# A decoder layer's down router: the hidden activations stored token by token and streamed, the router's table loaded as weights

## The reference

```
def kmoe(x_flat, W_router, A, B, scale, bias, d_in1, d_in2, d_out1, d_out2, top_k):
    logits = x_flat @ W_router.T                 # 64 experts
    vals, idx = jax.lax.top_k(logits, top_k)     # top_k = 2
    probs = jax.nn.softmax(vals, axis=-1)
    xs = x_flat.reshape(-1, d_in1, d_in2)
    Y = jnp.einsum('nkoi,nij,nkpj->nkop', A[idx], xs, B[idx])
    out = jnp.einsum('nkop,nk->nop', Y, probs).reshape(-1, d_out1 * d_out2)
    return out * scale + bias
...
h = kmoe(x_flat, W_up, A_up, B_up, scale_up, bias_up, 32, 32, 64, 64, 2)
h = jax.nn.gelu(h, approximate=False)
y = kmoe(h, W_down, A_down, B_down, scale_down, bias_down, 64, 64, 32, 32, 2)
```

## Time and profile before

| | |
|---|---|
| median of 3 runs | 1330.0 us (1328.71 to 1331.12) |
| the profiled execution | 1328.52 us |
| its span | 1326.8 us |
| mean granted TensorE clock | 0.972 |
| TensorE matmul busy | 1207.4 us, 91% |
| TensorE weight load busy | 968.3 us, 73% |
| ScalarE busy | 1086.1 us, 82% |
| VectorE busy | 962.7 us, 73% |
| GpSimd busy | 593.7 us, 45% |

### The profile page before, as it was taken

The page is one execution under the profiler, slowest core; times in us unless marked ns, Lnnn a source line. Parts: engine busy times, 40 slices in busy tenths (PEclk is TensorE's granted clock), DMA queues, the critical chain, the costliest instruction groups (busy, mean ns, idle before and its releaser), DMA issues.

```text
span 1326.8 us, 51823 instructions
## 1 busy us (share of the span) xinstructions
PE 1207.4 (91%) x16466; PEld 968.3 (73%) x16466; DVE 962.7 (73%) x3677; ACT 1086.1 (82%) x3158; POOL 593.7 (45%) x1846
## 2 busy tenths in 40 slices
PE   7899999999999999999999999999999999987535
PEld 6677787877777787777778777777878777775434
DVE  1466778696968879596877869597886969686634
ACT  2548888898988899898989889898888989887663
POOL 3112455362645546363544625354553626452432
PEclk9999999999999999999999999999999999998855
DMA  9200101010100101010010101001010101001000
GB/s 293 44 17 15 37 10 42 11 42 18 36 25 15 38 16 41 15 38 23 19 43 10 42 11 41 20 20 41 12 41 12 41 18 36 18 16 29 8 20 10
DMA packets 66209, 42.57 MB, mean 32 GB/s; under 512 B 18065, under 2 KB 64786, under 8 KB 65682
## 3 DMA queue, kind: packets, MB, share of 16 engines
q1 hardware_dynamic: 65938, 39.25, 10.6%
HBM read 34.98 MB, written 4.19 MB: 30 GB/s over the span
## 4 chain that ended last, share of the span: by engine, by line
PE 54%; DVE 16%; SPq 11%; issue 10%; ACT 4%; DMA 2%; DVEq 1%; POOL 0%; ACTq 0%; POOLq 0%
SPq L478 10%; PE P L804 5%; PE P L770 4%; PE PT L827 4%; PE P L781 4%; PE X L864 4%; PE PT L864 4%; PE P L757 3%; PE F L944 3%; DVE own L1131 3%; PE X L851 3%; DVE chosen_dn L418 3%; PE G L903 3%; PE S L820 3%; PE F L969 2%
## 5 line engine op out<-in xcount | busy, mean ns | idle before, releaser
L418 POOL COPY chosen_dn<-experts 64x64 f32 x1000 | 222.1, 278 | 218.5 <-issue 149.1
L659 ACT ACTIVATE probs<-probs,neg_max 128x128 f32<-128x128 f32 (+1 forms) x512 | 226.4, 444 | 23.1 <-DVE neg_max L1090 19.9
L404 POOL COPY chosen_up<-experts 32x128 f32 x512 | 181.9, 355 | 105.0 <-POOL chosen_up L404 51.9
L404 ACT COPY chosen_up<-experts 32x128 f32 x528 | 156.1, 296 | 17.0 <-DVE offsets L1175 4.2
L1090 DVE CUSTOM_DVE_ANT_0 probs<-S,distance 128x128 f32<-128x128 f32 (+1 forms) x512 | 151.9, 351 | 13.4 <-PE S L820 9.8
L827 PE MATMUL PT<-ident,probs 128*128 128x128 f32 x768 | 135.6, 286 | 10.4 <-DVE probs L1108 7.5
L698 ACT ACTIVATE hT<-h 64x1024 f32<-64x1024 f32 x64 | 126.7, 1980 | 7.6 <-DVE h L1221 6.2
L1108 DVE TENSOR_TENSOR probs<-probs,rinv 128x768 f32<-128x768 f32 x128 | 128.6, 1005 | 4.4
L770 PE MATMUL P<-ctxT,wk 128*128 128x256 f32 x512 | 121.0, 380 | 2.1 <-DVE x L1068 2.1
L781 PE MATMUL P<-wv,ctxT 128*128 128x256 f32 x512 | 122.5, 382 | 0.0
L1097 DVE COPY probsT<-PT 128x384 f32<-128x384 f32 x128 | 71.2, 557 | 69.5 <-PE PT L827 68.3
(11 more groups left out here) (131 smaller groups left out, 2822.0 us busy)
## 6 DMA issues: line engine op xcount, KB each, us to landing
chosen_up<-in_experts_up SPq DMA_DIRECT2D x992, 16.0 KB, 1.7
x<-in_x SPq DMA_DIRECT2D x16, 256.0 KB, 2.7
ctxT<-in_ctxT SPq DMA_DIRECT2D x16, 256.0 KB, 3.0
out<-x2b SPq DMA_DIRECT2D x16, 256.0 KB, 2.2
experts<-in_experts_up SPq DMA_DIRECT2D x2, 1024.0 KB, 19.2
wk<-in_xWk SPq DMA_DIRECT2D x1, 1024.0 KB
wo<-in_xWo SPq DMA_DIRECT2D x1, 1024.0 KB
wv<-in_xWv SPq DMA_DIRECT2D x1, 1024.0 KB, 7.7
```

The costliest lines, as they stand in the source:

```text
L404: last = copy(to[row:row + D1, n * 2 * F1:(n + 1) * 2 * F1], experts_up[k][:, bass.ds(held[g % loaded(units), unit], 2 * F1)])
L418: last = copy(dst, src.rearrange("p (m c) -> p m c", m=2))
L659: act.activation(probs[:, e % 4, lo:hi], probs[:, e % 4, lo:hi], ACT.Exp, bias=neg_max[:, e % 4, rt:rt + 1], scale=-1.0, accum_out=rsum[:, ...
```

## The change

`hT` becomes 128 partitions x 64 tokens x 32 values, so ScalarE reads `h` and writes `hT` in runs that lie side by side. The router streams `hT[:, :, o]`, 64 values that lie 32 elements (128 bytes) apart, and loads `r_dn[:, o, :]` as weights. With that the logits come out with experts on partitions and tokens along the row, so the fold loads `parts` as weights and streams the identities, which turns them back.

```
-        hT = sb("hT", [P, F1 // 2, TOKENS])
+        hT = sb("hT", [P, TOKENS, F1 // 2])
...
-                        src = h[half * F1:(half + 1) * F1, :].rearrange("p (n h o) -> p h o n", h=2, o=F1 // 2)[:, oh]
-                        dst = hT[oh * F1:(oh + 1) * F1, :, half * TOKENS // 2:(half + 1) * TOKENS // 2]
+                        src = h[half * F1:(half + 1) * F1, :].rearrange("p (n h o) -> p h n o", h=2, o=F1 // 2)[:, oh]
+                        dst = hT[oh * F1:(oh + 1) * F1, half * TOKENS // 2:(half + 1) * TOKENS // 2, :]
...
-                    mm = pe.matmul(G[to:to + F1, 0:EXPERTS], hT[:, o, :], r_dn[:, o, :],
+                    mm = pe.matmul(G[to:to + F1, 0:EXPERTS], r_dn[:, o, :], hT[:, :, o],
...
-                pe.matmul(G[0:F1, EXPERTS:2 * EXPERTS], fold[:, :], parts[:, :], start=True, stop=True)\
+                pe.matmul(G[0:F1, EXPERTS:2 * EXPERTS], parts[:, :], fold[:, :], start=True, stop=True)\
```

## The result

The change makes the kernel slower, clear of the noise: 1357.03 us (median of 4 runs, 1355.58 to 1361.58) against 1329.47 us before (4 runs, 1328.71 to 1331.12). The ratio is 1.0208, with a 95% interval of 1.0186 to 1.0231, or 27.6 us more; whether the loss is more or less than 2%, the interval leaves open. The profiled execution took 1361.58 us, the longest of the four. It reaches its first router at 172.01 us where before it was 168.7 us. These 3.3 us aren't the change's: already the first gelu, the first step that the change touches, starts at 163.55 us instead of 160.24. They are a part of its excess over the execution of before.

The account below looks back on a forecast made before the run. TensorE was taken to set each turn's pace. Router +22.4 us, sequence 14 -0.1 and sequence 15 -3.5 gave +18.8 on the profiled 1328.5, so 1347.3; the median lies 1.5 above, so 1349 us, range 1323 to 1358.

Parts of the forecast that it names:

- rival A: Router: TensorE fetches strided values at full rate, so only the gain at the end counts: -3.9 us, 1326.1 us; chance 0.38.
- What bounds the kernel: Each turn: TensorE sets the pace, busy 73 of 76 us; ScalarE, busy 67 us, has some 9 us to spare.
- The gelu: ScalarE's four hT pieces per sequence: 1980 to 1050 ns each, 60 us less on ScalarE, 3.5 to 3.9 us saved overall.
- the cover of sequences 0 to 13: TensorE's work from wo.0 to turn2, at least 8.9 us, hides the gelu there, so its speedup gains 0.
- The stride's price: Router: TensorE pays for strided values as ScalarE does, so a stream takes twice as long, 108 ns.
- still two side by side: Router: two strided streams overlap fully, 57 ns per matmul against 31.9, 1.6 us more per sequence, 22.4 us over sequences 0 to 13.
- Lines of 16 bytes: Router: a documented rule penalises moving to another SBUF line each access; by it every turn is longer, by VectorE's rows none.
- Sequence 14: Router starts 1.79 us earlier and ends 1.6 later, so the copy of parts moves by -0.2 to 0 us.
- Sequence 15: Uncovered gelu saves 3.5 us on the chain; router at half clock already takes 53 ns per matmul, so the stride costs 0.
- The fold: Matmul behind the router: loading parts instead of fold as weights costs 0, between -0.1 and +0.1 us.
- C: Router: strided streams exclude each other, 4.9 us more per router than forecast, +72 us, 1402 us; chance of C or beyond 0.15.
- D: Between gelu and q: relief of ScalarE shortens turns by at most some 0.3 us, 4 us in all; chance 0.04, inside A's.

Follow-up runs that it names:

- the contiguous stream: The changed kernel, but the router streams 64 values side by side in hT instead of 128 bytes apart (sums not the reference's): 1325.39 us, ratio 0.9962 to the kernel before.
- the swap alone: The kernel before with only router and fold operands swapped (table as weights, hT streamed), hT in its old layout: 1329.67 us, ratio 0.9997.
- the run with the even products first: The changed kernel with the router's 16 even products first, then the 16 odd, so no two streams run side by side: 1400.81 us; kernel before, so reordered: 1355.72.

## Why the prediction was right, and where it was off

**The number.** The forecast was 1349 us and the measured time is 1357.0: slower, as said, but by 27.6 us where the sum gave 18.8. It lies 1 us inside the range, which was wide because it took in rival A too, and 1 us above the forecast's own range of 1344 to 1356. The router grew by 2.1 us, above the 1.3 to 2.0 that went with that range. So the mechanism was right, one term was too small, and that the time still lies in the range is in part luck.

**What bounds the kernel** held. The turn grew by 2.2 us, what the router grew by, and 57 us less work on ScalarE shortened no turn: with the contiguous stream the turns stay at 76.2 us and the whole kernel gains 5.7 us.

**The gelu** held: 1055 ns against 1050. That the cover of sequences 0 to 13 makes it worth nothing is shown by the timeline after (hT ready 4 us early, ScalarE waiting).

**The stride's price** was right in kind. A strided stream takes 106 ns (the estimate, twice 54, was 108). The estimate went by likeness: TensorE asks for a value in 0.845 ns and ScalarE in 0.89, VectorE in 1.00. That it is this pace that decides which engine pays was argued and isn't shown; the number is no proof of it. In the last router, at a granted clock of 0.52 to 0.58, even contiguous streams come only every 53 ns (3.40 / 64), and there the stride costs less, 0.74 us for 2.1, which fits. The step that was mis-sized is the next one, "still two side by side, 54 ns per matmul, with some of the 4.9 ns kept: 57 ns", which took the overlap of two strided streams as complete. It measured 64.7, so the term of 1.6 us per router is 2.1, and 14 x 1.6 = 22.4 is 14 x 2.1 = 29.3.

**Lines of 16 bytes.** The trace after shows 307 against 222 ns, and the runs at steps of 8, 12, 16 and 128 bytes show 2.04, 3.0, 3.9 and 4.1 us per router. The Trainium skill, "Advanced Engine Details and Errata", section "Memory Cachelines", states that SBUF has lines of 16 bytes and that two hits on each are needed to absorb the latency. TensorE's and ScalarE's rows agree with it. VectorE's strided copies, which pay nothing (408 against 409 ns), don't; they were not tried further, and why they pay nothing stays open.

**Sequence 14** was said to move the copy of `parts` by -0.2 to 0. From the start of `wo.1` to that copy it is 1270.46 - 1262.75 = 7.71 us after and 1236.18 - 1228.65 = 7.53 before: +0.2. The router starts 1.9 us earlier by this measure, and takes 2.0 longer. The row of before from which it is counted:

```profile
1228.65 3.62 PE L864 MATMUL PT<-wo,attnT 128*128 128x256 f32 x16
```

**Sequence 15**: the router was said to cost nothing at half clock. It took 4.14 us in the chain against 3.40 in the chain of before (3.38 in the timeline), so 0.74 of the 3.5 us were given back, and 2.7 are left. The chain of the changed kernel there, and busy time by stretch with the granted clock (0.52) third from the end:

```profile
1324.80 1.06 ACT hT L698
1325.99 4.14 PE G L903 x64
```

```profile
1325.00:1330.00 5.00, 4.01 (x64) 3.91 (x64) 0.00 (x0) 4.14 (x4) 0.00 (x0) 0.52 0.01 3
```

The prediction set "the rate that the stride would set" at 53 ns there, the same mis-sized term.

**The fold** cost nothing that can be told, as the swap alone shows.

Put together: 29.3 + 0.2 - 2.7 = 26.8 us, against 27.6 measured. Forecast was 18.8, so all but 1 us of the miss is in the two places where 57 or 53 ns stood for 65. The two profiled executions differ by more, 33 us: 3.3 us lie before the first gelu, and 1.7 between sequence 14's copy and sequence 15's gelu, which the swap alone shows as well.

**The rivals.** A (full rate) fell; its price for the gelu's gain, -3.9 us, was about right (-5.7 by the medians; the ratio's interval is -2.9 to -7.2 us). C (strided streams exclude each other) fell by the changed kernel's own router, 4.1 us and not 7, and by the run with the even products first. D, the relief of ScalarE shortening the turns, would have to show in the contiguous stream's run; its turns are as before, 76.2 us. D fell.

## What to carry to other kernels

When a strided access is moved from an engine with time to spare to the one that sets the pace, work out the price there first: here nearly 60 us saved on ScalarE were worth 3 to 6, and 2.1 us per router on TensorE were paid fourteen times in full. The better question is whether the stride must cost anybody: blocks of two float32 values (8 bytes) gave both engines nearly their full rate. To tell what an operand's stride costs, run the same kernel with that operand contiguous.

## What the runs showed of the hardware

- A stream of 64 float32 values 128 bytes apart holds TensorE for 106 ns, a contiguous one for 58 (spacing of matmuls into one half of a bank). With two side by side it is 64.7 ns against 31.9. Streamed values and weights pay alike: 4.1 us per router either way, and the weight loads go from 138 to 220 ns.
- Two values in 16 bytes are enough: a step of 8 bytes costs TensorE nothing (221 ns), and runs of two cost ScalarE 1092 ns where long runs take 1055 and single values 1980. A step of 12 bytes costs TensorE about half of what one of 16 bytes does (0.9 and 1.8 us per router). VectorE's copies of single values pay nothing (408 against 409 ns).
- The strided router's time doesn't follow TensorE's clock: it takes 4.1 us at full clock and 4.14 us at a granted 0.52, where the contiguous one takes 2.04 and, at 0.58, 3.40. The stride's price falls from 2.1 to 0.7 us.
